# Turning the gathered expert rows on VectorE by way of a DRAM scratch, instead of on TensorE

## The reference

```
x = x + tanh(g_xattn) * (fake_quant(layernorm(x)) @ fake_quant(ctx))    # 512x1024 @ 1024x1024, per batch
y = layernorm(x)
logits = y @ W_gate + b_gate                       # 8 experts
top 2 experts of every token
x = x + tanh(g_ffn) * mean over the two of relu(y @ W_e[expert] + b_e[expert])   # W_e: 8 x 1024 x 1024
```

## Time and profile before

| | us |
|---|---|
| median of 3 runs | 419.95 (419.49 to 422.17) |
| the profiled execution, its own time | 422.89 |
| its span in the profile | 421.2 |
| PE busy | 327.9 (78%) |
| DVE busy | 228.7 (54%) |
| ACT busy | 137.1 (33%) |
| POOL busy | 147.3 (35%) |
| mean granted TensorE clock | 0.901 |

### The profile page before, as it was taken

The page is one execution under the profiler, slowest core; times in us unless marked ns, Lnnn a source line. Parts: engine busy times, 40 slices in busy tenths (PEclk is TensorE's granted clock), DMA queues, the critical chain, the costliest instruction groups (busy, mean ns, idle before and its releaser), DMA issues.

```text
span 421.2 us, 6706 instructions
## 1 busy us (share of the span) xinstructions
PE 327.9 (78%) x1680; PEld 258.5 (61%) x1687; DVE 228.7 (54%) x294; ACT 137.1 (33%) x115; POOL 147.3 (35%) x147
## 2 busy tenths in 40 slices
PE   0029488696853439999997997999999999999950
PEld 0014256263643438888886785888888877888840
DVE  1796875268896918435966753076222921862210
ACT  1565466615532007004551700071002600700000
POOL 2422654492588021122214412223133322533320
PEclk9999978898955558999999699899999999999995
DMA  4993121489259245935999596459444994444442
GB/s 150 406 389 154 51 100 52 169 358 321 100 205 340 105 137 191 321 78 123 310 362 396 174 337 165 100 125 391 138 100 96 267 374 102 111 95 100 98 95 50
DMA packets 23869, 81.46 MB, mean 193 GB/s; under 512 B 4017, under 2 KB 4017, under 8 KB 23857
## 3 DMA queue, kind: packets, MB, share of 16 engines
q1 hardware_dynamic: 15792, 54.56, 34.7%
q0 software_dynamic: 6192, 22.55, 23.5%
q10 hardware_dynamic: 1872, 4.20, 2.5%
HBM read 62.43 MB, written 18.87 MB: 193 GB/s over the span
## 4 chain that ended last, share of the span: by engine, by line
PE 52%; DVE 17%; DMA 12%; issue 7%; ACT 5%; POOL 1%; DVEq 1%; SPq 1%; POOLq 1%; ACTq 0%
PE ps L953 40%; DMA out_dram<-res,sidx 4%; PE ps_y L930 4%; PE ps L847 3%; DMA stage<-in_L_ffn_W_e_dram 3%; DVE lnv L600 3%; DMA xt<-in_x_dram 2%; DMA y_rows<-y_scratch,gidx 2%; PE ps L833 2%; DVE st L584 2%; PE ps_s L881 1%; PE ps_q L822 1%; DVE xt L625 1%; ACT y L451 1%; DVE lnv L601 1%
## 5 line engine op out<-in xcount | busy, mean ns | idle before, releaser
L953 PE MATMUL ps<-w_hi,yT_hi 128*128 x320 | 102.8, 403 | 3.1 <-issue 2.5
L953 PE MATMUL ps<-w_lo,yT_hi 128*128 x320 | 100.8, 397 | 0.0
L953 PE MATMUL ps<-w_hi,yT_lo 128*128 x320 | 100.4, 395 | 0.0
L805 DVE TENSOR_TENSOR res<-ps,bias 128x1024 f32<-128x1024 f32 x20 | 24.5, 1224 | 111.0 <-PE ps L953 110.1
L528 ACT ACTIVATE yT_hi<-ps_y 128x1024 fp32r<-128x1024 f32 x21 | 21.6, 1027 | 189.1 <-PE ps_y L930 189.1
L953 PEld LDWEIGHTS ps<-w_hi,yT_hi 128*128 128x128 f32 x320 | 60.1, 193 | 15.5 <-issue 4.1
L953 PEld LDWEIGHTS ps<-w_lo,yT_hi 128*128 128x128 f32 x320 | 61.4, 192 | 13.2
L953 PEld LDWEIGHTS ps<-w_hi,yT_lo 128*128 128x128 f32 x320 | 61.3, 192 | 13.2
L779 DVE TENSOR_TENSOR w_lo<-stage,w_hi 128x2048 f32 x28 | 62.6, 2287 | 8.5 <-ACT w_hi L544 8.2
L375 POOL COPY gidx<-idx 128x1 uint32 x23 | 4.6, 201 | 145.7 <-issue 101.5
L544 ACT ACTIVATE w_hi<-stage 128x2048 f32 x28 | 51.7, 1907 | 6.0 <-DMA stage<-in_L_ffn_W_e_dram 6.0
(11 more groups left out here) (120 smaller groups left out, 313.3 us busy)
## 6 DMA issues: line engine op xcount, KB each, us to landing
stage<-in_L_ffn_W_e_dram SPq DMA_DIRECT2D x32, 1024.0 KB, 8.5
stage<-in_ctx_dram SPq DMA_DIRECT2D x16, 512.0 KB, 8.8
xt<-in_x_dram SPq DMA_DIRECT2D x8, 512.0 KB, 10.3
y_scratch<-y ACTq DMA_DIRECT2D x8, 512.0 KB, 2.6
bias<-in_L_ffn_b_e_dram SPq DMA_DIRECT2D x8, 512.0 KB, 6.0
out_dram<-xt SPq DMA_DIRECT2D x8, 512.0 KB, 3.1
y_rows<-y_scratch,gidx POOLq DMA_INDIRECT x23
out_dram<-res,sidx POOLq DMA_INDIRECT x20, 6.3
```

Of the source, the lines that this page charges most:

```text
L805: dve.tensor_tensor(res[q][:, :], ps[q][:, :], bias[:, bass.ds(woff >> 3, D)], ALU.add).then_inc(s_free, 1)
L953: last = pe.matmul(ps[q][:, h * 512:(h + 1) * 512], lhs[q][:, k, :], w[:, bass.ds(woff + k * D + h * 512, 512)], start=(k == 0 and lhs is ...
```

## The change

- The gathered rows of a slot no longer go to TensorE. SP stores them from SBUF to a DRAM tensor `slot_scratch` (L284 of the new file, 512 KB, one transfer), waits for that, and reads them back with four transfers (L288) into a new tile `spread` of 128 x 4 x 256. Each of them fills a quarter of the partitions, with runs of 1 KB. There is one `spread`, so SP first waits until VectorE has turned the slot before (`s_tr`).
- VectorE turns `spread` in blocks of 32x32 (L822) into `yT_f`, which lies where `yT_lo` lies. ScalarE makes `yT_hi` from `yT_f`, VectorE subtracts in place. Both now read SBUF and not PSUM.
- So that block-wise turning gives whole columns, the first stage writes `y` with its columns in another order (`p (a k c)`), and `wg` is loaded in the same order, by eight transfers instead of one.
- SP's loop now runs over slots. In each step stand the row store, the four reads, the bias and, where `NXT` is set, the next weights. POOL's gather of slot+3 now waits for the store of slot+1 (`s_gd`) where it waited for the transposes.
- Many small tensors are moved to other addresses to make room. This moves no instruction.

```diff
+            def load_w(n, c, src):
+                sp.wait_ge(s_hi, n * NCH - NCH + c + 1)
+                settle(sp)
+                sp.wait_ge(s_lo, n * NCH - NCH + c + 1)
+                sp.dma_start(stage[:, CK * c:CK * (c + 1), :], src).then_inc(s_w[c], 16)
+            def store_rows(q):
+                sp.dma_start(slot_dram[q], y_rows[q][:, :]).then_inc(s_gd, 16)
+            def spread_rows(q):
+                for a in range(NQ):
+                    sp.dma_start(spread[QW * a:QW * (a + 1), :, :],
+                                 slot_dram[q].rearrange("(t i) (a c) -> a i t c", i=QW, a=NQ)[a]).then_inc(s_sp, 16)
...
+            def step(slot, q, turn):
+                sp.wait_ge(s_g[q], turn * 16 + 32)
+                settle(sp)
+                store_rows(q)
+                sp.wait_ge(s_gd, slot * 16 + 48)
+                settle(sp)
+                sp.wait_ge(s_tr, slot + 2)
+                spread_rows(q)
+                nxt = entry(sp, NXT, slot, E - 1)
+                with sp.If(nxt > 1):
+                    sp.wait_ge(s_post, slot)
...
+                with sp.If(nxt > 0):
+                    with sp.If(nxt < E - 1):
+                        n = sp.snap(entry(sp, NXT, slot, E - 2, lo=1) + 1)
+                        for c in range(NCH):
+                            load_w(n, c, w_t[:, bass.ds(n, 1), CK * c:CK * (c + 1), :].rearrange("p e k h -> p (e k) h"))
...
             def step(slot, q, turn):
-                pool.wait_ge(s_tp, slot + 2)
+                pool.wait_ge(s_gd, slot * 16 + 32)
                 gather(slot + 3, 1 - q, slot * 2 + 4)
...
-                act.wait_ge(s_tp, slot + 2)
+                act.wait_ge(s_tr, slot + 2)
                 act.wait_ge(s_mm, slot + 1)
-                evacuate_hi(slot + 1, 1 - q)
+                split_y_hi(1 - q)
...
+            def transpose_slot(q):
+                dve.transpose(yT_f[q][:, :, :].rearrange("p k (a c) -> p a k c", c=QW),
+                              spread[:, :, :].rearrange("p a (k c) -> p a k c", c=QW)).then_inc(s_tr, 1)
+            def split_y_lo(q):
+                dve.tensor_tensor(yT_lo[q][:, :, :], yT_f[q][:, :, :], yT_hi[q][:, :, :].bitcast(f32),
                                   ALU.subtract).then_inc(s_el, 1)
...
             def step(slot, q, turn):
+                dve.wait_ge(s_sp, slot * (16 * NQ) + 32 * NQ)
+                dve.wait_ge(s_mm, slot + 1)
+                transpose_slot(1 - q)
                 dve.wait_ge(s_eh, slot + 2)
-                evacuate_lo(1 - q)
+                split_y_lo(1 - q)
...
             def step(slot, q, turn):
-                pe.wait_ge(s_g[1 - q], turn * 16 + (16 if q == 0 else 32))
                 pe.wait_ge(s_el, slot + 1)
-                transpose_slot(1 - q)
```

More of the change, by code:

```diff
@@ L43, in flamingo_gated_moe @@
     w_t = W_e.rearrange("e (k p) h -> p e k h", p=P)
+    NQ = 4
+    QW = P // NQ
+    RW = D // NQ
     y_dram = nc.dram_tensor("y_scratch", (NT * P, D), f32, kind="Internal").ap()
@@ L70, in flamingo_gated_moe @@
         y_rows = [at(f"y_rows{q}", [P, D], f32, GB + 4 * KB * q) for q in range(2)]
+        yT_f = [at(f"yT_f{q}", [P, KT, P], f32, YT + 8 * KB + 4 * KB * q) for q in range(2)]
+        spread = at("spread", [P, NQ, RW], f32, SPR)
+        yT_f = [at(f"yT_f{q}", [P, KT, P], f32, YT + 8 * KB + 4 * KB * q) for q in range(2)]
+        slot_dram = [nc.dram_tensor(f"slot_scratch{q}", (P, D), f32, kind="Internal").ap() for q in range(2)]
         res = [at(f"res{q}", [P, D], f32, RES + 4 * KB * q) for q in range(2)]
@@ L243, in _ @@
                 load_x(i)
-            sp.dma_start(wg[:, :, :], W_gate.rearrange("(k p) e -> p k e", p=P)).then_inc(s_wg, 16)
+            wg_src = W_gate.rearrange("(h b a c) e -> b c a h e", h=KT // NQ, b=NQ, a=NQ)
+            for b in range(NQ):
+                for h in range(KT // NQ):
+                    sp.dma_start(wg[b * QW:(b + 1) * QW, :, :].rearrange("p (a h) e -> p a h e", a=NQ)[:, :, h, :],
+                                 wg_src[b][:, :, h, :]).then_inc(s_wg, 16)
             for k in range(KT, 2 * KT):
@@ L280, in _ @@
                     sp.nop()
                 sp.nop()
+            slots(sp, step)
         @block.gpsimd
@@ L769, in _ @@
             dve.wait_ge(s_tab, 1)
-            def evacuate_lo(q):
-                dve.tensor_tensor(yT_lo[q][:, :, :], ps_y[:, :, :], yT_hi[q][:, :, :].bitcast(f32),
+            def transpose_slot(q):
[3 more added lines that the diff above has]
+                dve.tensor_tensor(yT_lo[q][:, :, :], yT_f[q][:, :, :], yT_hi[q][:, :, :].bitcast(f32),
                                   ALU.subtract).then_inc(s_el, 1)
@@ L926, in _ @@
             last.then_inc(s_idx_ps, 1)
-            def transpose_slot(q):
-                for k in range(KT):
-                    last = pe.transpose(ps_y[:, k, :], y_rows[q][:, k * P:(k + 1) * P], ident_f[:, :])
-                last.then_inc(s_tp, 1)
             pe.wait_ge(s_tab, 1)
```

97 lines of the change are left out of this document (51 added, 46 removed).

## The result

The changed kernel takes **477.55 us** (median of 4 runs, 476.98 to 479.66) against 420.03 us, a ratio of **1.137, 95% interval 1.132 to 1.142**. It is slower, as forecast, but by 57.5 us where 25 were forecast, and 477.55 lies outside the range of 419 to 461. The profiled execution has a span of 477.9 us against 421.2, 56.7 us more.

A forecast was written before the change was run, and what follows sets the result against it. POOL's round and PE were taken as nearly equal bounds. Terms of -5.4 (transposes leave PE), +6.0 (later start) and +24.7 (stores beside scatters) gave +25.3 us on 419.95, so 445 us, range 419 to 461.

The forecast's parts named there:

- The start of the stage, +6.0: First slots of the expert stage: store, reads and VectorE's transpose make the first scatter 6.0 us later.
- The turn itself, 1.2 us: VectorE's transpose of a slot's 128x1024 float32 tile, taken as 1.2 us from a similar operation.
- The row store beside the scatter, +24.7: POOL's rounds: each 512 KB store falls on a scatter and adds 1.3 us, 19 x 1.3 = +24.7.
- the upper bound of 2.1: POOL's rounds: the most a store was taken to add to one round, 2.1 us.
- The reads and the order on VectorE and ScalarE, taken as 0: Slot loop: four reads covered by a two-slot lead, extra VectorE and ScalarE work hidden behind POOL's round; 0 us.
- The slack of -5.4: Expert loop: of 17.4 us of transposes leaving PE, at most 5.4 us reach the end, POOL's true slack.
- rival D: POOL's rounds lose more than 1.3 us each, possibly also through the new `yT_lo`: 460 us, chance 0.10.
- Rival C: PE and SP's queue set the pace, stores behind weights losing 3.5 us at six loads: 430 us, chance 0.20.
- What the prediction said would prove it wrong: POOL waiting for VectorE's results in most rounds, its round staying at 10.5 us, or a transpose of several us.

The follow-up runs named there:

- e13: Kernel before with the row store and four reads issued but unused, cut to 16 columns from the third slot on, waits kept: 438.06 us, 1.035.
- e16: Kernel before with unused row store in full and only the four reads cut to 16 columns from the third slot on: 446.76 us, 1.059.
- e4: Kernel before with row store and four reads carried in full but unused, POOL's gather also waiting for the store: 455.28 us, 1.079.
- e11: Changed kernel with VectorE turning the gathered rows directly, store and reads carried in full but unused: 457.87 us, 1.079.
- e14: Changed kernel, every instruction and wait kept, store and four reads cut to 16 columns from the third slot's rows on: 455.53 us, 1.077.
- e8: Changed kernel with two small transfers, one behind the other, between a slot's store landing and its reads: 550.14 us, 1.306.
- e9: Changed kernel without store and reads, VectorE turning 32x32 blocks straight from the gathered rows: 429.77 us, 1.017.
- e6: Kernel before with POOL waiting for a scatter's landing just ahead of the next scatter, not behind its own: 407.18 us, 0.966.
- e2: Changed kernel with each weight load of the loop cut to 16 columns of one row: 451.02 us, 1.071.
- e1: Changed kernel with the later experts' weights issued from ScalarE's queue instead of SP's: 473.15 us.
- e10: Changed kernel without store and reads, VectorE turning gathered rows directly, POOL's landing wait moved ahead of the next scatter: 411.61 us, 0.977.

## Why the prediction was wrong

Put in ratios against before, times 421 us, the runs make a ladder from the kernel before to the changed one:

| step | run | ratio | us added |
|---|---|---|---|
| the trip's order on SP and POOL, hardly any bytes, unused | e13 | 1.035 | 15 |
| the store's bytes | e16 | 1.059 | 10 |
| the reads' bytes | e4 | 1.079 | 9 |
| VectorE turns instead of TensorE | e11 | 1.079 | 0 |
| VectorE waits for the trip | changed | 1.137 | 24 |

The size of a rung depends on the order in which they are climbed. By way of e14 (1.077) the turn and the waiting add 18 us to e13 while the trip has hardly any bytes, and the bytes then add 25.

By the prediction's own steps:

- **The start of the stage, +6.0: right in the sum, with some luck.** First scatter at 179.82, forecast 179.5; +6.3. But the first gather was issued 2.6 us earlier than before (144.45 against 147.00), and from there to the first scatter it took 8.8 us more, not 6.0: the store landed in 4.1 us instead of 2.6, and the first slot's matmuls took 13.7 instead of 12.3.
- **The turn itself, 1.2 us: right**, 1.244 us. The estimate from the Trainium skill (VectorE: DVE Perf Modes, its section on the three transpose paths) of 2.5 us, worked out from bf16 figures, would have been twice too high.
- **The row store beside the scatter, +24.7: right in kind, too large for what it names.** The store's bytes cost 10 us by the ladder. POOL's own need did rise by 18.7 us, and by 33.4 in e4, but these sums are near 24.7 by luck: 9.7 us of the 18.7 are index copies that took longer (19.2 us against 9.5), and the 33.4 hold the reads' bytes and the new order on SP, both put at nothing. Nor was the price 1.3 us in each round. It is 0.34 in a quiet round and several us where weights move; the upper bound of 2.1, taken from a single scatter, was no bound.
- **The reads and the order on VectorE and ScalarE, taken as 0: this is the step that failed.** "Their cover is the two slots by which they run ahead" and "hidden behind POOL's round". POOL's true waits for results rose from 5.4 to 36.8 us, +31.4, which is nearly the whole miss of 32. Where the same trip runs but nothing waits for it they stay near the old value, 6.0 in e4 and 5.2 in e13. e8 shows that there was no such cover (3.6 us per slot for about 5 added), and the last rung of the ladder prices it at 24 us. The lead of two slots has to hold the gather, the store and the reads, and SP serves them in one order with the weights. For slot 7 the gather was issued at 236.16, the store, behind SP's issues of bias and weights, at 245.84, its landing took 14.90 us among 4 MB of weights, and the turn began at 268.45: 32.3 us, where two rounds of POOL are about 25 (12.4 each before). The prediction had the order on VectorE as 2.3 us of work in seven slots. It missed that a slot's result stands behind the next slot's turn, so that late reads also delay the scatter, and with it the gather that has to build up the next lead.
- **The slack of -5.4: eaten.** In e9, with PE relieved and no trip, the true waits fall from 5.4 to 1.5 us, but the kernel is 7 us slower than before, as POOL's small copies take 13 us more. The prediction had this effect only as an addition to rival D, with one copy of 1.37 us, and priced it at nothing in the sum. It expected the new `yT_lo` to do it; in e9 and in the change nearly all of it is `w_lo`.
- **Rival C** described many of the stretches that cost most, PE idle behind a weight load because the store queued behind it. It was put at 3.5 us for each of six loads, while four single gaps of PE were 9 to 11.4 us. And it was set against the forecast as another way to go, with the larger of two bounds deciding. They are one loop over several slots: scatter landing, gather, store, reads, turn, and behind the turn the result of the slot before and its scatter. A delay in one part is then not hidden by the other. Forecast and C's 3.5 x 6 together would have given 445 + 21 = 466 us.
- **What the prediction said would prove it wrong** did: POOL waits for VectorE's results in most rounds, ten of 19. The quiet round, forecast at 11.8 us, is 10.81.

What stays open: of the 15 us that the trip's order costs without bytes, some 6 are the late weight load, and the copies lengthened by 12 us (3 of them in a round that waited for VectorE anyway), which would be the rest; but no run takes the copies out of POOL's round, so this split is read from one trace. Freeing the gather of the store gave 5 us by the ratios, with intervals that touch, and moving the weights was tried only with all bytes. How the bytes raise a scatter's landing, by the engines' share or by order within them, was not parted either.

## What to carry to other kernels

Before you count a transfer as hidden, add up its whole way, with what the issuing engine does in between and the large loads ahead of it in the queue, and set that against the lead; the lead is used up exactly when the loads come. Then look at what stands behind the transfer in the order of the engine that waits for it: here a finished slot's result. Where two near-equal bounds hand work to each other, do not just take the larger. Count the small copies on a serial round too: they took up to ten times as long when they fell beside an operation with two inputs in SBUF. A wait that a profile puts down to a transfer should be checked against the count that the program waits for. And relieve the tighter one first: moving one wait behind three small issues on POOL gave 14 us (e6), while taking 17 us off TensorE gave none.

## What the runs showed of the hardware

- The same 512 KB store landed in 2.65 us (e8), 5.33 (e2, hardly any weights), 7.43 (e1, weights in another queue) and 14.90 (changed kernel, behind 4 MB of weights in its own). Changing the queue halves it and hands the rest to the transfer behind it.
- 4 MB of weights with a store behind them kept the DMA share at 0.96 to 1.00 for 18 us, at 328 to 338 GB/s. Half a megabyte more in such a stretch finds no free engine.
- POOL's 128-number index copies took 0.18 to 0.20 us beside an idle VectorE, beside its block transpose and beside `yT_lo` made from PSUM. Beside `w_lo`, with two inputs in SBUF, they took 0.65 to 2.33 us (e9), and beside `yT_lo` made from SBUF 0.52 to 1.66 (e10).
- A VectorE transpose in 32x32 blocks of a 128x1024 float32 tile takes 1.244 us, as long as an addition of that size (1.223 us, `res`).
- After a gap of 10.70 us TensorE's granted clock was 0.50, which is 1.2 of 2.4 GHz (changed kernel, 247.5 to 250 us; two matmuls in 1.05 us instead of 0.62), for some 4 us, which lengthened a slot by about 2 to 3 us. Each gap so costs more than its length.
